# Third wide attention of a decoder kernel: mix on four array parts, key projection on two row halves, division on POOL, norm pass on ACT, another order of work

## The reference

```python
q = rope(x @ wq.T)                 # 16 heads x 64
latent = x @ w_kv_down.T           # 64
k = rope(latent @ w_k_up.T)        # 16 heads x 64
v = latent @ w_v_up.T
p = softmax(q k^T / 8 + causal)
x = layernorm(x + concat(p v) @ wo.T)
```

## Time and profile before

| what | value |
|---|---|
| median of 3 runs | 1622.76 us (1622.22 to 1625.02) |
| the profiled execution's own time | 1620.42 us |
| its span | 1618.6 us |
| PE busy | 1291.4 us (80%) |
| DVE busy | 1168.8 us (72%) |
| ACT busy | 725.8 us (45%) |
| POOL busy | 824.2 us (51%) |
| mean granted PE clock | 0.922 |

### The profile page before, as it was taken

One profiled execution on the slowest core, in us unless ns is written; L12 is line 12 of the kernel. 1 busy time (PEld: TensorE's weight loads), 2 busy tenths in 40 slices (PEclk: granted clock), 3 DMA queues, 4 the chain that ended last, 5 costly groups with the idle time before them and its releaser, 6 DMA issues.

```text
span 1618.6 us, 41193 instructions
## 1 busy us (share of the span) xinstructions
PE 1291.4 (80%) x15406; PEld 876.6 (54%) x15406; DVE 1168.8 (72%) x2520; ACT 725.8 (45%) x1486; POOL 824.2 (51%) x1030
## 2 busy tenths in 40 slices
PE   7989869886878868779999788893888883898871
PEld 4556536556645547456666455681555543465540
DVE  6977858984688856568898577434788853798875
ACT  3544435544555544234444354250556521355555
POOL 4543357761377644435453364326557624456654
PEclk9999989997999989879999999795999987899995
DMA  9000000000000000000000000123000012000000
GB/s 340 1 1 1 0 0 0 0 1 22 0 1 0 0 1 14 0 7 1 0 0 1 1 0 3 44 56 132 1 0 1 0 42 35 3 0 2 0 1 26
DMA packets 19559, 29.95 MB, mean 19 GB/s; under 512 B 4291, under 2 KB 16323, under 8 KB 18714
## 3 DMA queue, kind: packets, MB, share of 16 engines
q1 hardware_dynamic: 17562, 24.97, 4.5%
q0 software_dynamic: 1920, 3.94, 1.4%
HBM read 23.91 MB, written 4.98 MB: 18 GB/s over the span
## 4 chain that ended last, share of the span: by engine, by line
PE 41%; DVE 23%; issue 15%; POOL 13%; ACT 6%; DMA 1%; POOLq 1%; DVEq 0%; ACTq 0%; SPq 0%
PE ps L333 32%; DVE maxima L430 6%; PE ps L453 4%; DVE arena L432 4%; PE ps L825 3%; POOL inv_norm L905 3%; ACT arena L440 3%; DVE heads_out L765 2%; POOL arena L910 2%; POOL arena L525 2%; DVE sq_sum L1039 1%; POOL arena L1940 1%; DVE gate L1795 1%; POOL arena L2228 1%; POOL rstd L371 1%
## 5 line engine op out<-in xcount | busy, mean ns | idle before, releaser
L333 PE MATMUL ps<-arena 64*64 64x64 f32 (+5 forms) x7921 | 381.8, 279 | 22.0 <-ACT arena L1222 4.7
L333 PEld LDWEIGHTS ps<-arena 64*64 64x64 f32 (+4 forms) x7921 | 236.2, 134 | 152.7 <-issue 122.3
L525 POOL TENSOR_TENSOR arena<-arena,w_const 128x1024 f32<-128x1024 f32 x96 | 182.3, 1901 | 151.7 <-DVE arena L755 66.7
L430 DVE TENSOR_REDUCE maxima<-ps 128x16 f32<-128x1024 f32 (+1 forms) x144 | 158.5, 1101 | 56.5 <-PE ps L333 52.6
L440 ACT ACTIVATE arena<-arena 128x1024 f32<-128x1024 f32 (+1 forms) x144 | 138.5, 962 | 127.9 <-DVE arena L432 127.0
L453 PE MATMUL ps<-w_const,arena 128*128 128x128 f32 x1024 | 144.1, 283 | 50.8 <-ACT arena L440 34.0
L905 POOL TENSOR_TENSOR inv_norm<-sq_floor,minus_half 128x16 f32<-128x16 f32 x32 | 121.9, 3810 | 86.4 <-DVE sq_floor L1042 86.2
L432 DVE TENSOR_TENSOR arena<-ps,maxima 128x1024 f32<-128x1024 f32 (+1 forms) x144 | 159.3, 1106 | 4.9
L447 ACT COPY arena<-ps 128x1024 f32<-128x1024 f32 (+1 forms) x144 | 131.4, 912 | 56.2 <-PE ps L453 55.7
L453 PEld LDWEIGHTS ps<-w_const,arena 128*128 128x128 f32 x1024 | 116.3, 144 | 74.0 <-ACT arena L440 44.2
L371 POOL TENSOR_TENSOR rstd<-var_eps,minus_half 128x1 f32<-128x1 f32 x144 | 80.5, 570 | 140.7 <-DVE var_eps L873 100.4
(11 more groups left out here) (317 smaller groups left out, 2649.7 us busy)
## 6 DMA issues: line engine op xcount, KB each, us to landing
experts<-in_pack_moe SPq DMA_DIRECT2D x2, 4180.0 KB, 20.3
w_fa<-in_pack_fa SPq DMA_DIRECT2D x2, 1024.0 KB, 11.2
moe_in<-state SPq DMA_DIRECT2D x2, 1024.0 KB, 5.4
w_a<-in_pack_a SPq DMA_DIRECT2D x1, 1824.0 KB, 18.0
moe_out<-arena SPq DMA_DIRECT2D x5, 256.0 KB, 3.5
w_fg<-in_pack_fg SPq DMA_DIRECT2D x2, 537.0 KB, 11.9
ctxT<-in_ctxT SPq DMA_DIRECT2D x1, 1024.0 KB, 7.4
out<-state SPq DMA_DIRECT2D x4, 256.0 KB, 2.3
```

Source lines behind the costliest of these rows:

```text
L333: return nc.tensor.matmul(o, lhsT, rhs, start=start, stop=stop, skip_group_check=True)
L430: nc.vector.reduce_max(mx, sc, X_AXIS).then_inc(signal["max_ready"], 1)
L525: nc.gpsimd.tensor_tensor(keys_wide(s).rearrange("p (b h t) -> p b h t", b=SEQS, h=8), key8(s).rearrange("p (b t) -> p b t", b=SEQS).unsqu ...
```

## The change

In `L1_ATTN` alone: (1) the mix goes parity first, and for the second sequence its output lands on the other 64 partitions, so that the four products use four different 64x64 parts; the scores of the second sequence are written with neighbouring heads exchanged to make up for it. (2) The down projection's weights stand twice side by side, so that the latent comes out on all 128 partitions; the key projection uses rows 0 to 63 for one half of the columns and rows 64 to 127 for the other. (3) `normal_probs` moves from DVE (lag 2) to POOL (lag 3). (4) The norm pass becomes a POOL product (`ln_bias`) and an ACT pass. (5) Score moves from lag 2, near the front of PE's step, to lag 1 at its end; `softmax_vector` moves to lag 1 at the end of DVE's step; the other pieces change places, as the `step` functions show. (6) DVE's `add` waits for the last tile but one to be done.

```diff
-        latentT = [shT[s][0:S, :] for s in STREAMS]
+        latentT = [shT[s][:, :] for s in STREAMS]
...
-        def score_wide(t, s, heads, keys):
+        def score_wide(t, s, heads, keys, swapped=()):
...
-                        last = mm(ps[s][b * S:(b + 1) * S, 2 + par, j * S:(j + 1) * S],
+                        at_head = j ^ 1 if b in swapped else j
+                        last = mm(ps[s][b * S:(b + 1) * S, 2 + par, at_head * S:(at_head + 1) * S],
...
-        def normal_probs(t, s, heads):
+        def normal_probs(eng, t, s, heads):
...
-            nc.vector.tensor_tensor(per_head, per_head,
-                                    inv_sum[s][:, 0:heads].unsqueeze(2).broadcast_to([P, heads, S]),
-                                    ALU.mult).then_inc(signal["heads_normal"], 1)
+            eng.tensor_tensor(per_head, per_head, inv_sum[s][:, 0:heads].unsqueeze(2).broadcast_to([P, heads, S]),
+                              ALU.mult).then_inc(signal["heads_normal"], 1)
...
+                def norm_bias(t, s):
+                    norm_pool(t, s)
+                    t.wait("ln_rstd", s, alone=True)
+                    nc.gpsimd.tensor_scalar(ln_bias[s][:, :], moments[s][:, 0:1], rstd[s][:, 0:1], -1.0,
+                                            ALU.mult, ALU.mult).then_inc(signal["ln_bias"], 1)
+
                 def step(tile):
                     for t, s in tile(0):
                         stage(t, s)
+                    for t, s in tile(3):
+                        normal_probs(nc.gpsimd, t, s, 16)
+                    for t, s in tile(4):
+                        norm_bias(t, s)
                     for t, s in tile(1):
                         key_sum(t, s)
-                    for t, s in tile(4):
-                        norm_pool(t, s)
                     for t, s in tile(0):
                         query_sum(t, s)
...
-                    mm(ps[s][0:S, 1, 0:P], part("a1", "down"), xT[s][:, :]).then_inc(signal["latent_projected"], 1)
+                    mm(bank(s, 1, 0, P), part("a1", "down"), xT[s][:, :]).then_inc(signal["latent_projected"], 1)
...
                     for k in range(2):
-                        last = mm(bank(s, k), latentT[s], part("a1", "k_up")[0:S, k * 512:(k + 1) * 512])
+                        rows = slice(k * S, (k + 1) * S)
+                        last = mm(bank(s, k), latentT[s][rows, :], part("a1", "k_up")[rows, k * 512:(k + 1) * 512])
...
-                    score_wide(t, s, 16, keyT(s))
+                    score_wide(t, s, 16, keyT(s), swapped=(1,))
...
-                    for b in range(SEQS):
-                        for par in range(2):
+                    for par in range(2):
+                        for b in range(SEQS):
                             rows = slice(par * S, (par + 1) * S)
-                            last = mm(ps[s][rows, 2 + b, :], latent_keys(s)[rows, b, :], probs_of[rows, :, b, :])
+                            turned = slice((par ^ b) * S, ((par ^ b) + 1) * S)
+                            last = mm(ps[s][turned, 2 + b, :], latent_keys(s)[rows, b, :], probs_of[rows, :, b, :])
...
                     for t, s in tile(3):
                         turn_probs_pe(t, 16, streams=(s,), ready="heads_normal")
-                    for t, s in tile(2):
-                        score(t, s)
                     for t, s in tile(0):
                         compress(t, s)
                     for t, s in tile(1):
                         turn_queries(t, s)
                     for t, s in tile(0):
                         project_queries(t, s)
+                    for t, s in tile(3):
+                        mix(t, s)
                     for t, s in tile(1):
                         turn_keys(t, s)
                     for t, s in tile(3):
-                        mix(t, s)
+                        output(t, s)
+                    for t, s in tile(0):
+                        project_keys(t, s)
                     for t, s in tile(1):
                         project_latent(t, s)
-                    for t, s in tile(0):
-                        project_keys(t, s)
-                    for t, s in tile(3):
-                        output(t, s)
+                        score(t, s)
...
+                def norm(t, s):
+                    t.wait("ln_bias", s)
+                    nc.scalar.activation(tile_of(state, t, s), total[s][:, :], ACT.Identity,
+                                         bias=ln_bias[s][:, 0:1], scale=rstd[s][:, 0:1]).then_inc(tile_done, 1)
+
                 def step(tile):
                     for t, s in tile(0):
                         turned_x(t, s)
-                    for t, s in tile(0):
                         latent(t, s)
+                    for t, s in tile(4):
+                        norm(t, s)
                     for t, s in tile(3):
                         probsT_scalar(t, 16, streams=(s,))
                     for t, s in tile(1):
                         queries(t, s)
+                    for t, s in tile(3):
+                        heads_mixed(t, s)
                     for t, s in tile(2):
                         exp_scalar(t, 16, 0.125, streams=(s,))
                     for t, s in tile(1):
                         keys(t, s)
-                    for t, s in tile(3):
-                        heads_mixed(t, s)
-                    for t, s in tile(1):
                         values(t, s)
...
                     t.wait("y_ready", s)
+                    t.wait_last(s)
...
                 def step(tile):
-                    for t, s in tile(2):
-                        softmax_vector(t, 16, streams=(s,))
                     for t, s in tile(0):
                         rotate_queries(t, s)
-                    for t, s in tile(4):
-                        norm_tile(t, s)
                     for t, s in tile(2):
                         row_sums(t, s, 16)
-                        normal_probs(t, s, 16)
                     for t, s in tile(3):
                         add(t, s)
+                        sum_statistics(t, s)
                     for t, s in tile(0):
                         rotate_keys(t, s)
-                    for t, s in tile(3):
-                        sum_statistics(t, s)
+                    for t, s in tile(1):
+                        softmax_vector(t, 16, streams=(s,))
...
-    packs["a1"] = {"wqk": i["L1_attn_wq"].T, "down": i["L1_attn_w_kv_down"].T,
-                   "k_up": rows_to(i["L1_attn_w_k_up"].T, P), "wv": chunked(by_parity(i["L1_attn_w_v_up"].T, 16, 64).T),
+    packs["a1"] = {"wqk": i["L1_attn_wq"].T, "down": np.concatenate([i["L1_attn_w_kv_down"].T] * 2, axis=1),
+                   "k_up": np.concatenate([i["L1_attn_w_k_up"].T] * 2, axis=0), "wv": chunked(by_parity(i["L1_attn_w_v_up"].T, 16, 64).T),
```

More of the change, by code:

```diff
@@ L82 @@
     "heads_turned": (L0_CROSS,), "headsT_ready": WIDE + (L0_CROSS,), "y_ready": FINISHED,
-    "resid_ready": NARROW + GLU + (L0_CROSS,), "ln_bias": NARROW + (L0_CROSS,), "sums_ready": WIDE + (L0_CROSS,), "gate_exp": (L0_CROSS,), "gate_den": (L0_CROSS,), "gate_ready": (L0_CROSS,),
+    "resid_ready": NARROW + GLU + (L0_CROSS,), "ln_bias": NARROW + (L0_CROSS, L1_ATTN), "sums_ready": WIDE + (L0_CROSS,), "gate_exp": (L0_CROSS,), "gate_den": (L0_CROSS,), "gate_ready": (L0_CROSS,),
     "paths_diff": (L0_CROSS,), "diff_gated": (L0_CROSS,),
@@ L1066, in step @@
                         row_sums(t, s, 8)
-                        normal_probs(t, s, 8)
+                        normal_probs(nc.vector, t, s, 8)
                     for t, s in tile(1):
@@ L1147, in project_latent @@
                             last = mm(ps[s][par * S:(par + 1) * S, 0, b * S:(b + 1) * S],
-                                      xT[s][:, b * S:(b + 1) * S], part("a1", "down"))
+                                      xT[s][:, b * S:(b + 1) * S], part("a1", "down")[:, 0:S])
                     last.then_inc(signal["v_projected"], 1)
@@ L1203, in latent @@
                     t.wait("latent_projected", s)
-                    nc.scalar.copy(latentT[s], ps[s][0:S, 1, 0:P]).then_inc(signal["latent_ready"], 1)
+                    nc.scalar.copy(latentT[s], bank(s, 1, 0, P)).then_inc(signal["latent_ready"], 1)
                 def queries(t, s):
```

## The result

| | before | after |
|---|---|---|
| median of the runs | 1622.49 us (6 runs) | 1611.27 us (6 runs, 1605.48 to 1616.68) |
| ratio | | 0.9928, 95% interval 0.9905 to 0.9951 |
| the profiled execution's own time, span | 1620.42, 1618.6 us | 1610.44, 1608.6 us |
| mean granted PE clock | 0.922 | 0.919 |

0.9928 of 1622.5 is 11.7 us less, with 7.9 to 15.4 as the interval. The forecast was 22 (1600.5 us, 1595 to 1613): right in sign and inside the range, twice too large in size, and outside the interval of the ratio. That it lies inside the range is partly luck: the range reached to 1613 for the sake of a longer steady step, and the steady step came out as forecast.

A forecast was written before the change was run, and what follows sets the result against it. PE alone bounds the stage; its new step (11.15) meets a loop of 11.2, taken as 11.3. 13 x (12.87 - 11.3) = 20.4, less 1.6, plus 3.4, saves 22.2 us: forecast 1600.5, range 1595 to 1613.

The forecast's parts named there:

- Part 1, the mix: PE's mix on four array parts: 1.98 us falls to 1.0, gain 0.95 a tile, bounds 0.85 and 0.
- Rival C: PE's mix stays at two parts because row tiles cannot share a bank: step 12.2, about 1614 us; chance 12%.
- Part 2, the keys: PE's key projection on two row halves: 1.91 us falls to 0.96, gain 0.95, bounds 1.0 and 0.
- PE's sum: PE's step: 12.76 - 1.90 = 10.86, plus a 0.25 to 0.3 stall ahead of the output: 11.15 us.
- the 0.11: Excess of the old mean step (12.87) over a steady step (12.76), from slow first transposes; carried into the 11.3 forecast.
- Part 3, the division: Division moved from DVE, where it takes 1.84, to POOL at 1.90 us, upper bound 2.38; both mutual waits go.
- Part 5, the loop: One-step loop through four engines, closed by POOL's division ahead of PE's turned probabilities: 11.2 us, 11.7 with division at 2.38.
- Rival B: Loop longer, through a division of 2.1 to 2.4 or slower handovers: step 11.6 to 11.9, about 1607 us; chance 30%.
- The fill: Stage start: shared steps even within 2 us; tile 0's turned probabilities wait for the division, +1.6.
- rival D: No part runs beside another and the new order costs: step 13.2, +5.5, about 1628 us; chance 5%.
- The first full step: First of thirteen steps: no term of its own, reckoned within the 11.3 us mean.
- The drain: Stage end, 31.2 us before: last score a step earlier gives -5.2, added chain terms +1.8, net -3.4.

The follow-up runs named there:

- e2: Changed kernel with the mix of before (two array parts, heads not exchanged): ratio 0.9991, step 12.14 us.
- e5: Changed kernel with the key projection back on one row half: one run, 1624.65 us, step 12.15 us.
- e4: Changed kernel with the division back on DVE, behind the row sums and ahead of the residual sum: ratio 0.9980, step 12.29 us.
- e12: Changed kernel with the division on DVE, behind the residual sum instead of ahead of it: ratio 0.9958, step 12.12 us.
- e1: Changed kernel with the maximum pass first in DVE's next step instead of last in its step: ratio 0.9887, fill 46.2 us.
- e9: Changed kernel with the maximum pass first in DVE's next step and the division last in POOL's step before: ratio 0.9874, fill 44.2 us.
- e11: Changed kernel with e9's order, e10's idle products and 13 idle products at the end of PE's second and third fill steps: ratio 0.9838.
- e10: Changed kernel with 27 idle products in the waits of PE's last two steps: ratio 0.9903, drain 28.7 us.
- e3: Kernel before with only the two packings (mix on four parts, key projection on two row halves): ratio 0.9928, step 11.92 us.

## Why the prediction was right in the middle and wrong at the ends

- **Part 1, the mix:** 0.95 taken, 0.84 by e2. Right, 0.1 high. Four parts at once with two row halves in each bank work as well as the form of the earlier trace rows. The Trainium skill (TensorEngine Tiling (Array Packing), Gotcha 1: PSUM Pressure) would have kept the mix at its old length; here the row halves write other partitions of the shared bank, and no cost appeared (1.02 us start to start). Rival C is out.
- **Part 2, the keys:** 0.95 taken, 0.85 by e5.
- **PE's sum:** 11.15, and 11.3 with the allowance; 11.30 measured. The wait ahead of the output is there (turn_keys to output 1.20, where turn_queries with nothing to wait for takes 0.88: 0.3). But the agreement is partly luck. The two packings gave 0.2 less than was taken, and the 0.11 that covered it was meant for something else, the slow start of the stretch.
- **Part 3, the division:** 1.90 on the nose, and both mutual waits gone. The Trainium skill (GPSIMD Engine Reference, Instruction dispatch) has the 2.5 cycles per element from which the prediction's estimate of 2.13 came; the trace does not agree. That, in the new order, the division had to leave DVE is shown by e4 and e12, 0.8 to 1.0 a step.
- **Part 5, the loop:** reckoned at 11.2, with no room to PE; the trace leaves 0.4, so it was some tenths shorter. Rival B is out, by the rows of POOL and by e2: the mix lies outside this loop, and its 0.84 lengthened the step in full.
- **The fill failed: 4.1 of the missing 8.8.** The prediction said that the two maximum passes ahead of the other stage's statistics were even with what the first key projection and the moved score save, "within 2", and added 1.6 for the division. Measured 5.7 longer instead of 1.6. e1 shows the passes at 5.6 by themselves, e9 the division at 2.0. What they were set against was worth 1.9 (46.1 in the kernel before, 44.2 in e9), not 5. None of the rivals had a longer fill as its cause; only rival D carried a part of it.
- **The first full step failed.** Its own showed tile 0's transposes at the lower clock (1.91 for 1.04), and the forecast allowed 0.11 in each of 13 steps for it, 1.4 in all. In the kernel before the first step was 1.95 longer than the mean of the others, in the changed one 2.7, and the 0.11 was used up by the packings. Of the 2.7, 1.6 is PE's clock (12.8 in e9, 11.2 in e11, which keeps PE at work ahead of it); the order gave 1.2 (14.0 in after, 12.8 in e9).
- **The drain was mis-sized by 2.0:** 28.9 forecast, 30.9 measured, 28.7 with idle products. The last maximum began 8.9 after tile 13's turned probabilities, for 8.8 in the forecast; the chain behind it took 22.0 (19.8 in e10) for 20.1. Behind its waits PE worked the last mix and the last output at the lower clock, 2.3 us more in all; e10, which fills the waits, has both at the full clock. That e10 meets the forecast does not prove each of its terms: the old drain from which it started had a slow output of its own (3.41 for 2.05). By an estimate from these rows the added terms of 1.8 were up to 1 us too small.
- **Rival D's sum** in the prediction has a slip: 4 + 3.4 - 1.5 is 5.9, not 5.5. It changes no conclusion.
- **Left open:** how the 0.62 that the moves and the order gave beyond the packings splits among them, what the norm pass on ACT is worth by itself, and the scatter of some us outside the stage.

## What to carry to other kernels

Reckon fill and drain of a software pipeline with the same care as its step: put the pieces of both stages in each queue's order, and ask which piece of the old stage now stands behind one of the new. A rotation of the order that leaves the steady round unchanged is free there and can be worth several us at a seam; and where PE has had waits of some us ahead of its work, as here in fill and drain, reckon with that work at the lower clock, or try idle products in the wait. When an engine's list is cut, ask what the others allow: packing alone gave 0.8 of 1.42 us a step here. The rest came with the new order and the division off DVE; the new order with the division left on DVE has a longer step (12.1 to 12.3) than packing alone (11.92).

## What the runs showed that I had not expected

- The two packings alone (e3) give the same whole, 0.9928, as the full change: its better step (11.30 for 11.92) is nearly paid back by its worse fill (51.8 for 47.1).
- Idle products of 3 us ahead of the first full step made that step 1.6 us shorter than in e9 (11.2 for 12.8) and delayed nothing, since they lay in a wait; 27 in the drain took 2.2 us off it.
- A DVE division with both operands in SBUF took 1.23, 1.36 or 1.84 us, and POOL's copy 0.29 or 1.30, the longer times where the other engine's instruction ran at the same time.
